# Routed expert tiles with the bias product behind their transposes, and five call lists in another order, in a two-layer attention and MoE kernel on one Trainium2 core

## What is computed

```python
def reference(x, ctx, g_xattn, g_ffn):
    h = x + tanh(g_xattn[0]) * cross_attention(layernorm(x), ctx)   # both directions, sigmoid gate between the two results
    h = h + tanh(g_ffn[0]) * moe_top1(h)        # 8 experts, 256 -> 256 with bias, each token to its best expert
    h = h + tanh(g_xattn[1]) * rope_attention(layernorm(h), ctx)    # 16 heads of 16
    h = h + tanh(g_ffn[1]) * moe_top2(layernorm(h))                 # 8 experts, 256 -> 128 -> 256, gelu
    return h
```

## Time and profile before

| | us |
|---|---|
| three runs | 508.23, 509.6, 510.47 |
| median | 509.6 |
| profiled execution, its span and its own time | 511.0 |
| PE busy in it | 477.8 |
| VectorE, ScalarE, POOL busy | 356.3, 337.6, 271.8 |

### The profile page before, as it was taken

The page is one execution under the profiler, slowest core; times in us unless marked ns, Lnnn a source line. Parts: engine busy times, 40 slices in busy tenths (PEclk is TensorE's granted clock), DMA queues, the critical chain, the costliest instruction groups (busy, mean ns, idle before and its releaser), DMA issues.

```text
span 511.0 us, 11124 instructions
## 1 busy us (share of the span) xinstructions
PE 477.8 (94%) x3918; PEld 416.3 (81%) x3918; DVE 356.3 (70%) x897; ACT 337.6 (66%) x691; POOL 271.8 (53%) x337
## 2 busy tenths in 40 slices
PE   3999999989999988689986999999999999999996
PEld 3899999989988878667754678698797978888896
DVE  6677666996655648965655878776774886975485
ACT  3578897865676614343365598888787768678843
POOL 2426564574604277756267777828666455513355
PEclk9999999997999976689998599999999999999999
DMA  6689810012357433687847152040411403000001
GB/s 185 207 278 327 291 43 2 22 62 96 92 163 234 140 104 105 183 284 221 268 125 242 44 188 65 33 139 1 153 39 43 170 22 126 26 1 24 1 22 41
DMA packets 41975, 61.51 MB, mean 120 GB/s; under 512 B 5198, under 2 KB 22976, under 8 KB 41920
## 3 DMA queue, kind: packets, MB, share of 16 engines
q1 hardware_dynamic: 36064, 52.67, 32.1%
q0 software_dynamic: 1536, 4.20, 2.7%
q10 hardware_dynamic: 4320, 3.93, 2.2%
HBM read 26.21 MB, written 17.43 MB: 85 GB/s over the span
## 4 chain that ended last, share of the span: by engine, by line
PE 75%; DVE 6%; issue 5%; DMA 4%; SPq 4%; POOL 3%; ACT 2%; POOLq 0%; ACTq 0%; DVEq 0%
PE psum L389 17%; PE psum L390 14%; PE psum L391 14%; PE psum L627 5%; PE psum L396 5%; PE psum L556 4%; PE psum L598 4%; PE psum L615 4%; PE psum L557 1%; SPq L3075 1%; PE psum L567 1%; POOL yg L2828 1%; DMA st<-parts 1%; PE psum L636 1%; PE psum L546 1%
## 5 line engine op out<-in xcount | busy, mean ns | idle before, releaser
L2261 DVE TENSOR_REDUCE mpad<-psum 128x4 f32<-128x1024 f32 x64 | 76.6, 1220 | 18.1 <-PE psum L598 17.4
L1381 ACT ACTIVATE PT<-psum 128x1024 f32<-128x1024 f32 x64 | 64.0, 1026 | 19.6 <-PE psum L615 16.2
L2800 POOL TENSOR_TENSOR wA<-stage,wA 128x512 fp32r<-128x512 f32 x32 | 41.3, 1291 | 49.4 <-ACT wA L1428 46.7
L2330 DVE SCALAR_TENSOR_TENSOR xall<-psum,gat,xall 128x256 f32<-128x256 f32 x112 | 47.1, 476 | 10.5 <-PE psum L391 5.9
L2746 POOL TENSOR_SCALAR nm<-mv 128x2 f32<-128x2 f32 x32 | 7.9, 247 | 60.7 <-DVE mv L2005 50.9
L389 PE MATMUL psum<-wB,wA 128*128 128x256 f32 x128 | 39.1, 305 | 0.0
L389 PE MATMUL psum<-x4h,wB 128*128 128x256 f32 x128 | 37.7, 294 | 0.0
L627 PE MATMUL psum<-PT,vv 128*32 128x256 f32 x512 | 35.1, 393 | 1.3 <-ACT PT L1381 1.3
L2787 POOL TENSOR_TENSOR parts<-qp,parts 128x512 fp32r<-128x512 f32 x16 | 20.8, 1302 | 28.9 <-ACT parts L1374 28.8
L390 PE MATMUL psum<-wB,wA 128*128 128x256 f32 x128 | 35.9, 281 | 0.0
L391 PE MATMUL psum<-wB,wA 128*128 128x256 f32 x128 | 35.9, 280 | 0.0
(11 more groups left out here) (283 smaller groups left out, 1758.3 us busy)
## 6 DMA issues: line engine op xcount, KB each, us to landing
st<-parts SPq DMA_DIRECT2D x48, 256.0 KB
wt<-exp_d SPq DMA_DIRECT2D x30, 256.0 KB, 2.7
slots_d<-ys SPq DMA_DIRECT2D x3, 2304.0 KB
stage<-mats_d SPq DMA_DIRECT2D x21, 256.0 KB, 3.7
cx<-ctx_d SPq DMA_DIRECT2D x16, 256.0 KB, 3.4
xs<-slots_d SPq DMA_DIRECT2D x30, 128.0 KB, 3.0
y_d<-ys ACTq DMA_DIRECT2D x30, 128.0 KB, 3.0
qr<-qp SPq DMA_DIRECT2D x28, 128.0 KB
```

What stands on the lines that cost most here:

```text
L1381: e.activation(PT[:, i:i + 2, :, :].rearrange("p a k n -> p (a k n)"), ps2("ST", b, j).rearrange("p a n -> p (a n)"), ACT.Exp, scale=0.25) ...
L2261: e.tensor_reduce(mpad[:, :, 0:16].rearrange("p t (o a) -> p t o a", a=8)[:, :, :, j], ps2("max", b, j).rearrange("p o (t n) -> p t o n", ...
L2330: e.scalar_tensor_tensor(out=xall[:, b, t, :], in0=ps("dn", b, x)[:, t * 256:(t + 1) * 256], scalar=gat[:, b % 2, t, x:x + 1], in1=xall[:, ...
L2800: e.tensor_tensor(hlo[:, i, :], stage[:, n % 4, :], hh[:, i, :].bitcast(F32), ALU.subtract).then_inc(h_lo, 1)
```

## The change

1. moe_T issues its two transposes, waits for the allocation and the bias table, and issues the bias product (start=True), and only then signals. moe_w then has the two expert products alone (start=False).
2. c_out is split into one call for each half of the tokens.
3. All five lists are in another order, and the PE calls take other banks. The set of calls is the same.

The diff has some 2,700 lines, nearly all of them list lines. The functions:

```diff
                 o = take(at, "moe", n)
                 w.wait_ge(d_tile[n % NT], 32 * (n // NT + 1))
                 for k in range(2):
-                    last = e.transpose(o[:, k * 128:(k + 1) * 128], xs[:, n % NT, k * 128:(k + 1) * 128], ident[:, :])
+                    e.transpose(o[:, k * 128:(k + 1) * 128], xs[:, n % NT, k * 128:(k + 1) * 128], ident[:, :])
+                g, j = tile_at(n)
+                w.wait_ge(v_tile, NALLOC * g + 12)
+                w.wait_ge(v_bo, 3)
+                last = e.matmul(o[:, 256:512], sel[:, g, j:j + 1].broadcast_to([2 * E, 128]), eb_r[:, :], start=True, stop=False)
                 last.then_inc(t_xs, 1)
 
             def moe_w(n):
                 o = ps("moe", n)
                 w.wait_ge(a_xs, n + 1)
-                g, j = tile_at(n)
-                w.wait_ge(v_tile, NALLOC * g + 12)
-                w.wait_ge(v_bo, 3)
                 for k in range(2):
-                    e.matmul(o[:, 256:512], xsT[:, n % 2, k, :], wt[:, n % NT, k * 256:(k + 1) * 256], start=(k == 0), stop=False)
-                last = e.matmul(o[:, 256:512], sel[:, g, j:j + 1].broadcast_to([2 * E, 128]), eb_r[:, :], start=False, stop=True)
+                    last = e.matmul(o[:, 256:512], xsT[:, n % 2, k, :], wt[:, n % NT, k * 256:(k + 1) * 256], start=False, stop=(k == 1))
                 last.then_inc(t_moe, 1)
 
             def route_D(b, at):
@@ -628,13 +628,12 @@
                                         start=(k == 0), stop=(k == 1))
                 last.then_inc(t_O, 1)
 
-            def c_out(b, *at):
-                for t in range(2):
-                    o = take(at[t], "OT", b, t)
-                    w.wait_ge(a_O, 2 * b + 2)
-                    for hg in range(4):
-                        last = e.transpose(o[:, hg * 128:(hg + 1) * 128], OT[:, hg, t * 128:(t + 1) * 128], ident[:, :])
-                    last.then_inc(t_OT, 1)
+            def c_out(t, b, at):
+                o = take(at, "OT", b, t)
+                w.wait_ge(a_O, 2 * b + 2)
+                for hg in range(4):
+                    last = e.transpose(o[:, hg * 128:(hg + 1) * 128], OT[:, hg, t * 128:(t + 1) * 128], ident[:, :])
+                last.then_inc(t_OT, 1)
 
             def c_outT(b, at):
```

The start of PE's list, and SP's:

```diff
@@ -670,535 +669,543 @@
                                hl(base[f"p{i}"], lambda a: a[:, j * 256:(j + 1) * 256]), True, True)
                 last.then_inc(t_dn, 1)
 
-            fold(0, 0)
-            fold_g(0, 1)
-            ln_T("A", 0, 2)
-            proj("t0", 0, 3)
+            fold(0, 6)
+            fold_g(0, 3)
+            ln_T("A", 0, 1)
+            proj("t0", 0, 6)
             proj("vc", 0, 0)
-            scores(0, 0, 1)
+            scores(0, 0, 4)
             fold(1, 2)
-            fold_g(1, 3)
+            fold_g(1, 5)
             vc_sums(4)
-            proj("t1", 0, 2)
-            proj("vs", 0, 3)
-            ln_T("A", 1, 1)
-            scores(1, 0, 5)
...
+            load("qc")
+            load("vs")
+            small()
+            load("ks")
             for t in range(2):
                 e.dma_start(xall[:, 0, t, :], x_d[0][:, t, :]).then_inc(d_x[0], 16)
+            load("vc")
+            load_ctx("A", 0)
+            load_x(1)
             e.dma_start(ident[:, :], id_d).then_inc(d_id, 16)
-            load("qc")
-            small()
-            load("ks")
-            load_ctx("A", 0)
-            load("vs")
-            load("vc")
             load_x(2)
             tables()
             load("kc")
+            load_x(3)
+            load("g1")
+            zero_slots(0)
+            load_ctx("A", 1)
             load("qs")
-            load_x(1)
-            load("g1")
```

PE's list around the first group's ranks (104 to 122 us of the profile before), its added lines:

```diff
+            route_B(2, 1)
+            mix(3, 5)
+            proj("t1", 5, 2)
             proj("vs", 5, 7)
-            ln_T("B", 2, 0)
             P_T(1, 4, 3)
-            PV(0, 4, 1)
-            proj("vc", 5, 2)
-            PV(1, 4, 0)
-            rank(1, 1)
-            scores(0, 5, 3)
-            route_B(2, 0)
-            ln_T("B", 3, 1)
+            rank(1, 6)
+            rank(2, 4)
+            PV(0, 4, 5)
+            PV(1, 4, 3)
+            ln_T("B", 3, 6)
+            scores(0, 5, 1)
             scores(1, 5, 4)
-            route_B(3, 1)
-            proj("t0", 6, 0)
-            rank(2, 3)
-            rank(3, 1)
-            gate(4, 2)
-            P_T(0, 5, 3)
-            proj("t1", 6, 4)
-            P_T(1, 5, 5)
-            ln_T("A", 6, 1)
-            PV(0, 5, 3)
-            PV(1, 5, 5)
-            proj("vs", 6, 2)
-            proj("vc", 6, 0)
-            scores(0, 6, 1)
-            scores(1, 6, 3)
-            gate(5, 4)
-            mix(4, 1)
-            moe_T(0, 3)
-            proj("t0", 7, 5)
-            moe_T(1, 1)
+            route_B(3, 5)
+            proj("vc", 5, 7)
+            proj("t0", 6, 6)
+            ln_T("A", 6, 5)
+            rank(3, 0)
+            gate(4, 4)
+            scores(0, 6, 3)
+            P_T(0, 5, 5)
+            P_T(1, 5, 6)
+            proj("vc", 6, 2)
```

Around the second group's ranks and the last tiles (182.6 to 295.5 us):

```diff
             moe_w(14)
-            rank(4, 0)
-            route_B(5, 1)
-            gate(7, 2)
-            rank(5, 0)
-            mix(7, 1)
-            c_k(0, 2)
-            ln_T("B", 6, 0)
-            route_B(6, 1)
-            ln_T("B", 7, 0)
-            rank(6, 2)
-            ln_T("C", 0, 1)
-            route_B(7, 3)
-            c_q(0, 0)
-            rank(7, 1)
-            ln_T("C", 1, 2)
+            gate(7, 1)
+            ln_T("B", 6, 4)
+            route_B(5, 5)
+            route_B(6, 6)
+            mix(7, 2)
+            rank(4, 1)
+            rank(5, 2)
+            c_k(0, 5)
+            ln_T("B", 7, 7)
             c_v(0, 0)
-            c_q(1, 3)
-            c_k(1, 0)
-            c_v(1, 1)
-            moe_T(15, 0)
-            moe_T(16, 2)
+            ln_T("C", 0, 5)
+            rank(6, 7)
+            route_B(7, 6)
+            c_q(0, 2)
+            rank(7, 3)
+            ln_T("C", 1, 4)
+            c_k(1, 6)
+            c_v(1, 3)
+            c_q(1, 5)
+            moe_T(15, 6)
+            moe_T(16, 0)
+            moe_T(17, 2)
+            moe_T(18, 7)
             moe_w(15)
-            moe_T(17, 3)
             moe_w(16)
-            moe_T(18, 0)
             moe_w(17)
...
+            c_maxT(0, 2)
+            c_max(1, 1, 6)
             moe_w(25)
-            c_max(0, 1, 4)
-            c_max(1, 1, 6)
-            c_maxT(0, 1)
-            moe_T(26, 3)
-            c_k(3, 0)
+            c_max(2, 1, 3)
+            c_k(3, 1)
+            moe_T(26, 0)
+            c_max(3, 1, 6)
             moe_w(26)
-            c_max(2, 1, 4)
-            c_q(3, 1)
-            moe_T(27, 6)
-            c_max(3, 1, 4)
-            moe_T(28, 2)
+            moe_T(27, 4)
+            c_q(3, 5)
             moe_w(27)
-            c_max(4, 1, 4)
-            moe_T(29, 3)
+            moe_T(28, 6)
+            moe_T(29, 0)
+            c_exp(0, 0, 3)
             moe_w(28)
-            c_exp(0, 0, 6)
-            c_exp(1, 0, 4)
             moe_w(29)
+            c_max(4, 1, 1)
             c_max(5, 1, 6)
-            c_exp(2, 0, 4)
-            c_PV(0, 0, 0)
+            c_exp(1, 0, 3)
+            c_exp(2, 0, 0)
+            c_PV(0, 0, 3)
             c_exp(3, 0, 6)
             c_max(6, 1, 4)
-            c_exp(4, 0, 6)
+            c_exp(4, 0, 1)
+            c_max(7, 1, 6)
             c_PV(1, 0)
             c_exp(5, 0, 4)
             c_exp(6, 0, 6)
-            c_exp(7, 0, 4)
-            c_PV(2, 0, 1)
-            c_max(7, 1, 6)
+            c_exp(7, 0, 0)
+            c_maxT(1, 2)
+            c_PV(2, 0, 5)
             c_PV(3, 0)
-            c_v(3, 0)
-            c_out(0, 1, 2)
-            c_maxT(1, 3)
-            c_outT(0, 0)
-            c_max(0, 2, 4)
-            c_max(1, 2, 6)
-            c_wo(0, 1)
+            c_out(0, 0, 2)
+            c_out(1, 0, 4)
+            c_v(3, 3)
+            c_outT(0, 7)
+            c_max(0, 2, 0)
             c_exp(0, 1, 4)
+            c_exp(1, 1, 2)
+            c_max(1, 2, 5)
+            c_wo(0, 7)
+            c_exp(2, 1, 3)
+            c_exp(3, 1, 1)
             c_max(2, 2, 6)
-            c_exp(1, 1, 4)
-            c_exp(2, 1, 6)
-            c_exp(3, 1, 4)
             c_PV(0, 1, 0)
-            c_exp(4, 1, 6)
-            ln_T("C", 4, 1)
-            c_max(3, 2, 4)
+            c_max(3, 2, 3)
+            c_max(4, 2, 5)
+            ln_T("C", 4, 7)
             c_PV(1, 1)
-            c_max(4, 2, 6)
-            c_exp(5, 1, 4)
-            c_max(5, 2, 6)
-            c_exp(6, 1, 4)
-            c_PV(2, 1, 2)
-            c_exp(7, 1, 6)
+            ln_T("D", 0, 3)
+            c_exp(4, 1, 1)
+            c_max(5, 2, 5)
+            c_k(4, 4)
+            route_D(0, 0)
+            c_exp(5, 1, 5)
+            c_exp(6, 1, 1)
+            d_up(0, 0, 7)
+            c_PV(2, 1, 3)
+            c_exp(7, 1, 1)
+            c_q(4, 6)
```

(96 more changed lines are left out.)

1578 lines of the change are left out of this document (769 added, 809 removed).

## The result

The changed kernel takes 519.66 us (median of 4 runs, 516.35 to 521.8), the kernel before 510.04 us beside it. The ratio is 1.023, 95% interval 1.018 to 1.028: slower by 9.6 us, where 2.8 us less were forecast. Run again later beside the experiments it gave 518.39 us and 1.024 (1.017 to 1.030). Medians here are over all executions, while the ratios and their intervals leave out slow ones, over 1.5% above the fastest of their kernel, so a ratio can differ from the quotient of its two medians by up to 0.7%, and verdicts go by the ratios.

A forecast was written before the change was run, and what follows sets the result against it. PE, busy 94% of the span, bounds the kernel, through its waits and low clock. Terms +6.3 + 1.7 + 0.6 - 3.4 - 3.5 - 4.2 - 0.3 = -2.8 us from 509.6 give 506.8, rounded to 507.0 us; range 499.5 to 514.5.

The forecast's parts named there:

- Bias product: Bias product ahead of the expert products in 30 tiles: 0 us, weight loads still idle near 10 us.
- Start: fold(1) waits for load qs behind the zero fill, +6.3 us (0 to +7.6), then slow clock, +1.7 us (0 to +3).
- Banks, 20 to 100 us: New bank neighbours between 20 and 100 us cost some +0.6 us, 0 to +3.
- Region A: 104 to 122 us: wait and slow clock at rank(3) go, -4.9 us, later tiles take some back: -3.4 us (-5 to 0).
- Region B: 182.6 to 226.3 us: waits ahead of mix(7) and c_q(1) covered, clock regained, less waits for tiles: -3.5 us (-6 to 0).
- the tiles perhaps 2 us: Around tiles 15 to 18: PE comes 4 to 5 us earlier, the tiles perhaps 2; some 2.5 to 3 us becomes waiting.
- Between B and C: Stretch between the 182.6 to 226.3 and 262.6 to 295.5 us regions: loses one c_max of cover, gains one, -0.3 us.
- Region C: 262.6 to 295.5 us: maxima and c_exp earlier, half the idle and some slow clock go: -4.2 us (-6 to -2).
- signs that the prediction named for being right: fold(1) at 23.7 to 25.8 us, clock falling near 25; waits at rank(3), c_q(1), head_max(7,1) gone; bias idle near 10 us.
- those for being wrong: fold(1) at 18 us, tiles 15 to 18 waiting over 4 us, or PE idle above 3 us from 20 to 104 us.
- the slower one: Start and banks cost 13.6 us, the three later regions give only 7.5: +6 us, about 514 us; chance 0.25.

The follow-up runs named there:

- e3: Kernel before with the bias product moved behind the tile's transposes, lists and banks as before: 511.75 us, ratio 0.999.
- e4: Changed kernel with the bias product back behind the expert products, lists and banks as changed: 522.54 us, 1.017 against the kernel before.
- e13: The changed kernel run again, with no further edit: 518.39 us.
- e14: Changed kernel with load qs right behind kc, the zero fill behind ctx(A,1), and w_lo(vs) ahead of w_lo(vc): 511.55 us, 1.008 against the kernel before.
- e2: Kernel before with only its zero fill moved early, between loads kc and qs: 516.30 us, ratio 1.009.
- e10: Kernel before with gate(4) ahead of rank(3) on PE, nothing else: 512.94 us, ratio 1.004.
- e17: e14 with everything the engines had not begun by 306 us in the order and banks of the kernel before: 521.11 us, 1.018 against the kernel before.
- e9: Kernel before with head_max(7,1) and max_parts(1) earlier on VectorE, c_maxT(1) and c_exp(0,1) moved on PE: 511.17 us, ratio 1.003.
- e11: Kernel before with c_v(0), c_k(1), c_v(1) earlier on PE, ctx_lo(C,1) ahead of scatter(6) on POOL, ScalarE copies earlier: 509.04 us, ratio 1.000.

## Why the prediction was wrong

Forecast 507.0 us, range 499.5 to 514.5; measured 519.66. By its own steps:

- **Bias product, 0:** the number is right (e3, e4), the ground given for it only in part. The idle of the weight load was to stay near 10 us under its new line and is 5.4 us; neither these 5 us nor the whole 10.3 were worth anything to the end.
- **Start, +6.3 and +1.7:** the mechanism was right in each part, queue, wait and slow clock; undersized. fold(1) came at 25.95 us (24.5 taken, 23.7 to 25.8 bounded), in e13 at 24.59, and the lag is 10.4 us at 30 us, 0.9 of it since PE begins earlier. The slow clock was sized by half of one stretch of 3.5 us; it lasts 6.9 us here and 13.7 us in e13. Taken to the end the start is 6.8 us (e13 against e14), or 4.5 to 5.5 us put into the kernel before (e2).
- **Banks, 20 to 100 us, +0.6:** -0.8, below its bounds of 0 to 3.
- **Region A, -3.4:** the trace shows -5.3 up to 124 us and then +2.6 back up to 183, -2.7 in all, and the other profiles of the new order have the same -4.7 to -5.3. But e10 finds no gain from its main move. The step that failed is to count the low clock behind rank(3) in full against the order of before: behind the same wait it is there whole, by half or not at all, 1.5 us in the mean of six profiles where 3.0 were taken.
- **Region B, -3.5:** the lag falls 7.0 us up to 206 us and rises 6.9 us up to 226, net 0. The failed step is "the tiles perhaps 2 us" and, ahead of it, that c_k(1) and c_v(1) would cover the wait: I had POOL's new order in hand and did not ask what ctx_lo(C,1) stood behind.
- **Between B and C, -0.3:** +3.4 in this profile, and +0.3 in e13, +0.6 in e14, +2.4 in e17. c_max(0,1) now comes ahead of moe_w(25) and waits for stack(1), by 2.81, 1.03, 0.87 and 1.68 us. Where the lag grows most the granted clock is at 0.50 from that wait on (255.0 to 261.9 us here, 250.6 to 257.5 us in e17); in e13 and e14 it stays at 1.00.
- **Region C, -4.2:** -1.6 in the trace from 250 to 323 us, -1.5 in e13, -0.5 in e14, and e9 finds no gain when its moves are made alone.
- **Behind 300 us, not priced at all:** +1.3 behind 323. I took a dense stretch for one that can't get worse.

The failed step is thus that of the gains: A, B and C were added up to -11.1 us as if each wait taken out, with its low clock, stayed out. In the profile the regions from 108 to 323 us give -1.0 us, and e9, e10 and e11 give ratios of 1.003, 1.004 and 1.000 for the moves that carried them.

Most signs that the prediction named for being right did come (a wait for a stage load ahead of fold(1), clean region A, no wait at c_q(1)) and none of those for being wrong; they tested the single waits, not what would stand in their place.

The rival that came nearest is the slower one: the start decides and the chains of A, B and C move with PE. It was given 0.25. Its own sum, +6 us on 509.6, is 515.7 us and not 514, and still too low. It had 13.6 us for the start and the banks, where 9.6 came, gave A, B and C 7.5 us, where 1.0 came, and had nothing behind 300 us, so that it came near is in part luck.

By the medians the start is 6.8 us of the loss of 9.2. Of the rest the late order is 0.9 to 1.3 us; e14 still has 3.4 us of lag at 30 us, and what the remainder is made of is open. The regions that the prediction counted as gains come to nothing that can be told.

## What to carry to other kernels

Ahead of a load on which the whole machine waits, put no bulk transfer into the same queue; put it behind, and look at what the engines can do meanwhile. A wait that the trace names is not a gain until the next thing to arrive is named as well: in e11 the wait removed stood in front of one for a tile (slots, alloc, scatter), in e10 in front of two for VectorE and ScalarE, in e9 in front of c_exp's. Low-clock episodes in one profile are priced only after further profiles of the same code show them too, and at their mean.

## What was not expected of the hardware

The same code runs 5.4 us apart by 226 us in two profiles (the kernel before, and e9, whose edits lie behind 262 us), 3.0 us of it where one has the low clock behind rank(3) and the other does not: one and the same wait of 1.9 us was followed by 6.8, 3.4 or 0 us at 0.50. Runs of the kernel before lie between 503.67 and 517.38 us. And the 16-row weight load waits 0.17 us behind transposes and 0.34 to 0.36 us behind the expert products (5.0, 10.3 and 10.9 us over 30), though both have 128-row weights; no effect of it on the time can be told.
